# Constants and picked sums in PSUM, a first count split differently between two engines, and GpSimd's second threshold ahead of the spread scales

## The chip, the cores and the metric

The kernel runs on one core of one Trainium2 chip. Its time is the device time of one execution in microseconds (us), and runs of the same kernel are compared by their median. Before the change the median of three runs is 1032.03 us (1031.37 to 1032.18).

A core has five engines that work side by side, each in the order of its own instruction stream: TensorE (PE; the loading of its weights is shown as PEld), VectorE (DVE), ScalarE (ACT), GpSimd (POOL) and SyncE (SP), which here only starts transfers. They wait for each other by counting semaphores. SBUF is the large on-chip memory, PSUM the small one that TensorE writes its products to.

## The reference

Four sequences of 512 tokens with 128 features run through two layers. What matters here is the attention of the second layer: 16 heads, 16 memory keys in front of the 512 tokens, and of the scores of each query only the 64 largest go into the softmax.

```
dots = einsum('bhid,bhjd->bhij', q, k) * scale          # k has 16 memory keys in front
dots = einsum('bhij,hk->bkij', dots, pre_proj)          # heads mixed
dots = where(causal, neg, dots)
top  = lax.top_k(dots, 64)[0]
vk   = top[..., -1:]                                    # the 64th largest score of the row
dots = where(dots < vk, neg, dots)
attn = softmax(dots)
attn = einsum('bhij,hk->bkij', attn, post_proj)
out  = einsum('bhij,bhjd->bhid', attn, v) ... @ Wo + bo
```

Before it come a linear recurrence and a feed-forward part in simulated four-bit numbers, behind it a mixture of eight experts with a shared one. The change does not touch these.

## The kernel before

The work of attention is cut into 64 steps, one for each head of each sequence, numbered g from 0 to 63 (HEADS). In a step the 512 queries are four tiles of 128 rows (t = 0 to 3); because of the causal mask tile t needs only 144, 272, 400 or 528 columns of scores (NT). The mixing of heads is folded into weights ahead of the loop.

What a step does, and on which engine:

- TensorE computes keys (line 415) and scores (lines 438 to 441) of a later head, turns the weights of a head by a product with a scaled diagonal matrix `spread` (`turn_weights`, line 450, 20 matmuls), and multiplies them with the values (`values`, line 464).
- VectorE fetches the scores from PSUM into `Sx` (`fetch`, line 1025), measures their size (lines 1031 and 1036), and counts part of the entries over a first threshold (`tally`, line 1043).
- ScalarE counts the rest of them (`first_tally`, line 728), GpSimd corrects the threshold (`second_threshold`, lines 1313 to 1317), ScalarE counts again for all tiles (`tally`, line 736), and GpSimd corrects once more and shifts the scores by the result (`third_threshold` and `shift`, line 1334). ScalarE counts how many shifted scores are positive (`count`, line 744). The 64th largest score now lies within a few places of zero.
- VectorE finds out which side of zero it lies on (`flip`: `away`, line 1050, `flips`, line 1052, and the flipped scores, line 1056), takes the 8 nearest scores (`nearest`, line 1062), and picks the right one by a mask that GpSimd has made (`pick_last`, lines 1339 to 1344): product with the mask, line 1124, sum, line 1129, flip back into `yk`, line 1134. One matmul of TensorE (`found`, line 471) counts whether each row has its hit; VectorE reads that (`read_hits`, lines 1069 and 1070), and where a row has none it goes through a branch with the next 8 scores (`redo_missed`). `keep` (line 1111) zeroes the softmax weights under the limit and sums the rest; `rinv` (line 1114) is one over the sums.
- GpSimd multiplies the identity by `rinv` into `spread` (`spread_scale`, line 1353) and scales the weights of the memory keys (`mem_w`, line 1357). `turn_weights` waits for `spread`; ScalarE copies its result out of PSUM (`turned_copy`, line 763), and `values` waits for this copy.

The steps overlap: every engine works at several heads at a time. There is no scheduler. Each engine's order is written out in a loop over g with offsets. For ScalarE one pass is: `key_copy(g + 3)`, `tally(g + 1)`, `turned_copy(g - 1)`, `weigh(g + 1)` (the exponentials, line 755), `value_copy(g)`, `count(g + 1)`, `first_tally(g + 2)`. For TensorE: `turn_weights(g - 1)`, `found(g)`, `projected(g)` (line 422), `values(g - 1)`, `scores(g + 3)`, `keys(g + 4)`. For GpSimd: `second_threshold(g + 1)`, `pick_last(g)`, `stage_memory_keys(g + 3)`, `third_threshold(g + 1)`, `shift(g + 1)`, `first_threshold(g + 2)`, and last `spread_scale(g)` with the memory weights.

Of the kernel before, what the change touches and what calls it, by code (L numbers as in the profile page):

```python
# [5 lines left out]
I32 = mybir.dt.int32  # L6
BF16 = mybir.dt.bfloat16
ALU = mybir.AluOpType
# [3 lines left out]
P = 128  # L12
B, T, D = 4, 512, 128
TT = T // P
# [30 lines left out]
def mix_jobs():  # L45

    for i in range(2):
        for lo in range(0, PAIRS, 512):
            yield i, lo, min(PAIRS, lo + 512)
    yield 2, 0, 2 * D  # L50


ORDER = [(b, u) for pair in ((0, 1), (2, 3)) for us in (range(SH), range(SH, UNITS)) for b in pair for u in us]
# [12 lines left out]
def mixed_layers_kernel(nc, xT, W_in, b_in, log_A, B_vec, Cm, Dv, w_gate, w_up, w_down, WqT, WkT, WvT,  # L66
                        pre, post, memkT, memvT, Wo, bo, w12T, w3T, s1T, s2T, s3T, rwT, ebias, steer, outT):
    ctx = ExitStack()
    with ctx:
# [83 lines left out]

        y = [tiles_of(mixed_flat[:, STOT * i:STOT * i + STOT]) for i in range(2)]
        near = tiles_of(mixed_flat[:, 2 * STOT:3 * STOT])
        steer_s = sb("steer_s", [P, 6, TT])
        size = [sb(f"size{i}", [P, TT]) for i in range(2)]
        cf = [sb(f"cf{i}", [P, 5, TT]) for i in range(2)]
        moved = sb("moved", [P, TT])
# [43 lines left out]
        quad = [bA[:, :], bBC[:, 0:512], bBC[:, 512:1024], bI]  # L203
        scores_in = [bA[:, 0:NT[0]], bA[:, OFF[1]:OFF[1] + NT[1]], bBC[:, 0:NT[2]], bBC[:, 512 - MEM:1024]]
        hits_in = bA[0:1, 512 - 2 * TT * WIN:512].rearrange("p (t k) -> p t k", t=TT)
        ln4_bank = [bBC[:, 0:512], bBC[:, 512:1024], bA[:, :], bF]
        half_bank = [(bBC[:, 0:512], bI), (bA[:, :], bBC[:, 512:1024])]
        ln3_bank = [bH[:, :], bF, bG, bI]
# [55 lines left out]
        def _(pe):  # L264
# [306 lines left out]
            for g in range(-2, HEADS + 1):  # L571
                if g == 1:
                    pe.wait_ge(sem("ln_out"), 3 * B)
                if 0 <= g - 1:
                    turn_weights(g - 1)
                if g == HEADS:
                    wide4(0)
                    wide4(1)
                    pe.wait_ge(sem("hits_read"), HEADS)
                    mean4(2)  # L580
                if 0 <= g < HEADS:
                    found(g)
                    projected(g)
                if 0 <= g - 1:
                    values(g - 1)
                if g and g % H == 0:
                    turn_memory(g // H - 1)
                if 0 <= g + 3 < HEADS:
                    scores(g + 3)
                if g + 4 < HEADS:  # L590
                    keys(g + 4)
# [41 lines left out]
        def _(act):  # L633
# [89 lines left out]
            def first_tally(g):  # L723

                act.wait_ge(sem("fetched"), TT * (g + 1))
                act.wait_ge(sem("thr0_ready"), g + 1)
                for t in range(2, TT):
                    last = nc.scalar.activation(unread[1][:, OFF[t]:OFF[t] + NT[t]], Sx[g % 2][:, t, 0:NT[t]], ACT.Sign, bias=cf[g % 2][:, 0, t:t + 1],  # L728
                                                accum_out=above[:, t:t + 1])
                last.then_inc(sem("tallied0_last"), 1)  # L730
# [123 lines left out]
        def _(dve):  # L854
# [184 lines left out]
            def tally(g):  # L1039

                dve.wait_ge(sem("thr0_ready"), g + 1)
                for t in range(2):
                    last = V.tensor_scalar(unread[1][:, OFF[t]:OFF[t] + NT[t]], Sx[g % 2][:, t, 0:NT[t]], cf[g % 2][:, 0, t:t + 1], 0.0, ALU.is_ge, ALU.add,  # L1043
                                           accum_out=above[:, t:t + 1])
                last.then_inc(sem("tallied0"), 1)

            def flip(g):

                dve.wait_ge(sem("counted"), g + 1)
                V.tensor_tensor(away[:, :], over[g % 2][:, :], steer_s[:, 5, :], ALU.add).then_inc(sem("away_ready"), 1)  # L1050
                dve.wait_ge(sem("away_ready"), g + 1)
                V.tensor_scalar(flips[:, :], away[:, :].bitcast(I32), REST, TWO, ALU.bitwise_or, ALU.bitwise_xor).then_inc(sem("flips_ready"), 1)
                dve.wait_ge(sem("flips_ready"), g + 1)
                for t in (3, 2, 1, 0):
                    dve.wait_ge(sem("y_ready"), TT * g + 4 - t)
                    V.tensor_scalar(near[t].bitcast(I32), y[g % 2][t].bitcast(I32), flips[:, t:t + 1], None, ALU.bitwise_xor).then_inc(sem("flipped"), 1)  # L1056
# [15 lines left out]
            def redo_missed(g):  # L1072
# [3 lines left out]
                with dve.If(dve.value_load(hits[0:1, TT:TT + 1]) < TT * P):  # L1076
# [9 lines left out]
                    dve.drain()  # L1086
                    V.tensor_reduce(vk_far[:, :], further[:, :, :], AX.X, ALU.add)
                    dve.drain()
                    V.tensor_tensor(vk[:, :], vk[:, :], vk_far[:, :], ALU.add)
                    dve.drain()  # L1090
                    V.tensor_tensor(yk[:, :].bitcast(I32), vk[:, :].bitcast(I32), flips[:, :], ALU.bitwise_xor)
# [28 lines left out]

            def pick_tops(g):

                dve.wait_ge(sem("topped"), 2 * g + 2)
                V.tensor_tensor(picked_top[:, :, :], pick[:, :, 0:WIN], top[:, :, :], ALU.mult).then_inc(sem("top_picked"), 1)

            def add_tops(g):

                dve.wait_ge(sem("top_picked"), g + 1)
                V.tensor_reduce(vk[:, :], picked_top[:, :, :], AX.X, ALU.add).then_inc(sem("vk_ready"), 1)

            def last_kept(g):

                dve.wait_ge(sem("vk_ready"), g + 1)
                V.tensor_tensor(yk[:, :].bitcast(I32), vk[:, :].bitcast(I32), flips[:, :], ALU.bitwise_xor).then_inc(sem("yk_ready"), 1)  # L1134

            for g in range(-2, HEADS):
                there, coming = 0 <= g, g + 2 < HEADS
                if there:
                    flip(g)
                    nearest(g, (3, 2))  # L1140
                    nearest(g, (1, 0))
                    if g == 0:
                        for b in range(1, B):
                            normed(2, b, ln3_bank[b])
                    if g > H and g % H == 1:
                        take_sum(g // H - 1)
                    read_hits(g)
                if coming:
                    free_for_fetch(g + 2)
                    fetch(g + 2, (0,))  # L1150
                if there:
                    pick_tops(g)
                if coming:
                    fetch(g + 2, (1,))
                if there:
                    add_tops(g)
                if coming:
                    fetch(g + 2, (2,))
                if there:
                    last_kept(g)  # L1160
                if coming:
                    measure_first(g + 2)
                    fetch(g + 2, (3,))
                if there:
# [99 lines left out]
        def _(pool):  # L1264
# [33 lines left out]
            def first_threshold(g):  # L1298

                ph = g % 2  # L1300
                pool.wait_ge(sem("sized"), g + 1)
                if g >= 2:
                    pool.wait_ge(sem("counted"), g - 1)
                Gp.tensor_tensor(cf[ph][:, :, :], size[ph][:, :].unsqueeze(1).broadcast_to((P, 5, TT)), steer_s[:, 0:5, :],  # L1304
                                 ALU.mult).then_inc(sem("thr0_ready"), 1)
                Gp.tensor_scalar(nmax[ph][:, :], rmax[ph][:, :], -1 / DOWN, None, ALU.mult).then_inc(sem("nmax_ready"), 1)

# [38 lines left out]
            def spread_scale(g):  # L1346
# [4 lines left out]
                if g:  # L1351
                    pool.wait_ge(sem("turned_all"), g)
                Gp.tensor_tensor(spread[:, :, :], ident[:, :].unsqueeze(1).broadcast_to((P, TT, P)),  # L1353
                                 r[:, :].unsqueeze(2).broadcast_to((P, TT, P)), ALU.mult).then_inc(sem("spread_ready"), 1)
                if h == 0 and b:
                    pool.wait_ge(sem("memT_done"), b)
                Gp.tensor_tensor(mem_w[:, :, h, :], Ex[g % 2][:, :, 0:MEM], r[:, :].unsqueeze(2).broadcast_to((P, TT, MEM)), ALU.mult).then_inc(sem("mem_ready"), 1)

            for g in range(-3, HEADS):
                if 0 <= g + 1 < HEADS:  # L1360
                    second_threshold(g + 1)
                if g >= 0:
                    pick_last(g)
                if g + 3 < HEADS:
# [6 lines left out]
                if g == -1:  # L1371
                    pool.wait_ge(sem("ln_root"), 1)
                    for b in range(1, B):
                        Gp.tensor_tensor(diag3[b].rearrange("p (t n) -> p t n", t=TT), ident[:, :].unsqueeze(1).broadcast_to((P, TT, P)),
                                         rstd[:, TT * b:TT * b + TT].unsqueeze(2).broadcast_to((P, TT, P)), ALU.mult).then_inc(sem("ln_diag"), 1)
                if g >= 0:
                    spread_scale(g)
            for b in range(B):
                pool.wait_ge(sem("ln_root"), max(b, 1) + 1)
                Gp.tensor_tensor(diag4[b].rearrange("p (t n) -> p t n", t=TT), ident[:, :].unsqueeze(1).broadcast_to((P, TT, P)),  # L1380
                                 rstd[:, TT * b:TT * b + TT].unsqueeze(2).broadcast_to((P, TT, P)), ALU.mult).then_inc(sem("ln_diag"), 1)


def steering():

# [8 lines left out]
    for t in range(TT):  # L1394
        for p in range(P):
# [12 lines left out]
            slope = n * exp(-z * z / 2) / sqrt(2 * pi)  # L1408
            step = sigma / slope
            half = GAIN * step / 2  # L1410
            if t < 2:
# [45 lines left out]
```

## Time and profile before

| | |
|---|---|
| median of 3 runs | 1032.03 us |
| the profiled execution | 1033.08 us, its span 1031.4 us |
| PE busy | 909.6 us (88%) |
| DVE busy | 848.0 us (82%) |
| ACT busy | 746.8 us (72%) |
| POOL busy | 471.8 us (46%) |
| mean granted TensorE clock | 0.950 of full speed |

The span is the time from the first to the last instruction of that execution; what lies around it is 1.7 us. The shares are means over the whole kernel. The loop over heads lies at about 188 to 853 us and has other shares than its surroundings, so it has to be looked at by itself. An engine that is busy all the time within a stretch sets its pace there; where several are, each of them may. In the rows below, "idle before" is the time for which an engine had nothing to do in front of an instruction, and the name behind an arrow is what ended that time.

### The profile page before, as it was taken

What the parts mean: (1) busy time and instruction counts of PE and PEld (TensorE: products, weight loads), DVE (VectorE), ACT (ScalarE), POOL (GpSimd) and SP (SyncE); (2) the same over time, 40 slices, a digit from 0 to 9 for tenths busy, and PEclk for the clock granted to TensorE, in tenths of its full rate; (3) what the DMA queues carried; (4) which work ended last, traced back from release to release, by engine and by line L of the source; (5) the groups of instructions that cost most, each with busy time, mean ns of one, the idle gap of its engine ahead of it and who ended that gap; (6) DMA issues with size and microseconds to landing.
All of it is one profiled execution on the core that took longest, in us unless ns stands there. A gap on an engine that the chain in (4) does not pass through costs nothing.

```text
span 1031.4 us, 16155 instructions
## 1 busy us (share of the span) xinstructions
PE 909.6 (88%) x4151; PEld 581.7 (56%) x4151; DVE 848.0 (82%) x2863; ACT 746.8 (72%) x1932; POOL 471.8 (46%) x1113
## 2 busy tenths in 40 slices
PE   7856777998999998989999999789998789899998
PEld 4523444666666666666666666567666566433432
DVE  4687994999999999999999999989999983446344
ACT  6423236899999999999999999779998883211211
POOL 2000013677676676676766776556765652000000
PEclk9867988899999999999999999989999989899999
DMA  4855310000000000000000000000000000000000
GB/s 155 157 119 92 77 16 1 1 2 2 2 2 2 2 1 2 2 1 2 2 2 2 2 2 2 1 2 2 2 2 1 1 1 1 0 1 10 11 1 21
DMA packets 15006, 18.13 MB, mean 18 GB/s; under 512 B 2657, under 2 KB 12193, under 8 KB 14241
## 3 DMA queue, kind: packets, MB, share of 16 engines
q1 hardware_dynamic: 14880, 16.84, 7.7%
q14 instruction: 93, 0.75, 0.3%
q8 instruction: 33, 0.54, 0.2%
HBM read 11.07 MB, written 5.77 MB: 16 GB/s over the span
## 4 chain that ended last, share of the span: by engine, by line
DVE 48%; PE 28%; issue 11%; ACT 7%; POOL 2%; DVEq 1%; POOLq 1%; DMA 0%; ACTq 0%
DVE Ex L1111 11%; DVE top L1062 7%; DVE mixed L1056 6%; DVE Sx L1025 4%; DVE unread L1043 3%; PE bH L464 3%; DVE yk L1134 2%; PE bFGI L450 2%; PE bBC L559 2%; PE bA L559 2%; DVE away L1050 2%; PE bFGI L568 2%; PE bFGI L560 2%; PE bBC L560 2%; PE bH L568 2%
## 5 line engine op out<-in xcount | busy, mean ns | idle before, releaser
L1334 POOL TENSOR_TENSOR mixed<-Sx,nthr 128x528 f32<-128x528 f32 (+3 forms) x256 | 185.8, 757 | 11.5 <-issue 11.5
L450 PEld LDWEIGHTS bFGI<-spread,Ex 128*128 128x128 f32 x1280 | 157.4, 202 | 58.9 <-POOL spread L1353 57.5
L464 PE MATMUL bH<-turned 128*128 128x512 f32 (+3 forms) x512 | 152.9, 442 | 36.9 <-ACT turned L763 36.6
L450 PE MATMUL bFGI<-spread,Ex 128*128 128x128 f32 x1280 | 166.8, 289 | 17.4 <-POOL spread L1353 17.4
L736 ACT ACTIVATE unread<-Sx,nthr 128x144 bf16<-128x144 f32 (+3 forms) x256 | 143.9, 563 | 20.2 <-POOL nthr L1315 16.6
L464 PEld LDWEIGHTS bH<-turned 128*128 128x128 f32 x512 | 92.1, 189 | 97.9 <-issue 77.6
L744 ACT ACTIVATE unread<-mixed,least 128x528 bf16<-128x528 f32 (+3 forms) x256 | 143.4, 566 | 0.0
L1111 DVE SCALAR_TENSOR_TENSOR Ex<-mixed,yk,Ex 128x144 f32<-128x144 f32 (+3 forms) x256 | 139.5, 598 | 1.7 <-ACT Ex L755 1.0
L755 ACT ACTIVATE Ex<-Sx,nmax 128x144 f32<-128x144 f32 (+3 forms) x256 | 125.5, 563 | 0.0
L1062 DVE MAX8 top<-mixed 128x8 f32<-128x528 f32 (+3 forms) x256 | 110.8, 493 | 0.0
L1353 POOL TENSOR_TENSOR spread<-ident,rinv 128x512 f32<-128x512 f32 x64 | 66.5, 1039 | 84.1 <-DVE rinv L1114 84.1
L728 ACT ACTIVATE unread<-Sx,cf 128x400 bf16<-128x400 f32 (+1 forms) x128 | 85.7, 673 | 9.1 <-POOL cf L1304 9.1
L1056 DVE TENSOR_SCALAR mixed<-mixed,flips 128x528 int32<-128x528 int32 (+3 forms) x256 | 84.0, 390 | 2.3
L763 ACT ACTIVATE turned<-bFGI 128x1280 f32<-128x1280 f32 x64 | 77.8, 1216 | 11.0 <-PE bFGI L450 11.0
L1025 DVE CUSTOM_DVE_ANT_0 Sx<-bBC,causal 128x400 f32<-128x400 f32 (+1 forms) x128 | 79.7, 623 | 0.6 <-PE bBC L441 0.5
L422 PE MATMUL bE<-per_head,xn 128*128 128x128 f32 x512 | 76.9, 295 | 0.0
L441 PE MATMUL bBC<-Y,xn 128*128 128x512 f32 x128 | 71.7, 642 | 0.0
L422 PEld LDWEIGHTS bE<-per_head,xn 128*128 128x128 f32 x512 | 64.6, 198 | 7.9 <-issue 0.9
L415 PE MATMUL bE<-xn,per_head 128*128 128x512 f32 x128 | 65.5, 593 | 1.6 <-DVE xr L986 1.6
L438 PE MATMUL bA<-Y,xn 128*128 128x144 f32 (+1 forms) x256 | 57.4, 348 | 1.4 <-ACT Y L721 0.8
L1290 POOL COPY um_turned<-per_head 128x256 f32<-128x256 f32 x1 | 0.7, 736 | 126.4 <-DMA per_head<-mixed_store 126.4
L839 ACT ACTIVATE Ex<-bBC 128x512 f32<-128x512 f32 x24 | 14.3, 597 | 57.0 <-PE bFGI L560 57.0
(346 smaller groups left out, 1797.7 us busy)
## 6 DMA issues: line engine op xcount, KB each, us to landing
heads_store<-per_head SPq DMA_DIRECT2D x2, 1152.0 KB, 5.0
mixed<-heads_store SPq DMA_DIRECT2D x16, 144.0 KB, 10.8
mixed_store<-mixed SPq DMA_DIRECT2D x2, 1152.0 KB, 4.2
per_head<-mixed_store SPq DMA_DIRECT2D x16, 144.0 KB, 6.0
xr<-in_xT SPq DMA_DIRECT2D x4, 256.0 KB, 3.5
w_s<-in_w12T SPq DMA_DIRECT2D x1, 1024.0 KB, 13.9
outT<-xc SPq DMA_DIRECT2D x4, 256.0 KB, 2.0
wq_s<-in_WqT SPq DMA_DIRECT2D x1, 512.0 KB, 4.2
```

Of the source, the lines that this page charges most:

```text
L422: done = mm(bE[:, jt * P:jt * P + P], xn[:, b, jt * P:jt * P + P], Bw[:, h, :], start=True, stop=True)
L450: last = mm(bFGI[:, k * P:k * P + P], Ex[g % 2][:, t, a:a + P], spread[:, t, :], start=True, stop=True)
L464: last = mm(bH[:, jt * P:T], u[:, jt, :], PT[:, at:at + n], start=h + jt == 0, stop=False)
L728: last = nc.scalar.activation(unread[1][:, OFF[t]:OFF[t] + NT[t]], Sx[g % 2][:, t, 0:NT[t]], ACT.Sign, bias=cf[g % 2][:, 0, t:t + 1], accu ...
L736: last = nc.scalar.activation(unread[0][:, OFF[t]:OFF[t] + NT[t]], Sx[g % 2][:, t, 0:NT[t]], ACT.Sign, bias=nthr[g % 2][0][:, t:t + 1], ac ...
L744: last = nc.scalar.activation(unread[2][:, OFF[t]:OFF[t] + NT[t]], y[g % 2][t], ACT.Sign, bias=least[:, :], accum_out=over[g % 2][:, t:t + 1])
L755: nc.scalar.activation(Ex[g % 2][:, t, 0:NT[t]], Sx[g % 2][:, t, 0:NT[t]], ACT.Exp, bias=nmax[g % 2][:, t:t + 1], scale=1 / DOWN).then_inc ...
L1025: V.tensor_tensor_reduce(out=Sx[g % 2][:, t, 0:NT[t]], in0=scores_in[t], in1=causal[:, W - NT[t]:W], scale=DOWN, scalar=LOW, op0=ALU.add, ...
L1056: V.tensor_scalar(near[t].bitcast(I32), y[g % 2][t].bitcast(I32), flips[:, t:t + 1], None, ALU.bitwise_xor).then_inc(sem("flipped"), 1)
L1062: last = V.max(top[:, t, :], near[t])
L1111: V.scalar_tensor_tensor(Ex[g % 2][:, t, 0:NT[t]], y[g % 2][t], yk[:, t:t + 1], Ex[g % 2][:, t, 0:NT[t]], ALU.is_ge, ALU.mult, accum_out=r ...
L1334: Gp.tensor_tensor(y[ph][t], Sx[ph][:, t, 0:NT[t]], nthr[ph][1][:, t:t + 1].broadcast_to((P, NT[t])), ALU.add).then_inc(sem("y_ready"), 1)
```

## The change

There are three parts, and one thing that follows from them.

First, two operands of small VectorE operations come to lie in PSUM. `steer_p` holds the constants that `away` adds, copied there once ahead of the first head; `vk_p` holds the sums of the picked scores, which `yk` reads. Both lie in the bank `bA`, between the scores of tile 1 and the hits. Because the matmuls of the scores write the same bank, `flip(g)` now also waits until TensorE has done the first scores of head g + 2. The picking and its sum now stand directly behind `read_hits`, ahead of the fetches of head g + 2, and the flip back stands behind the first of the four fetches. In the branch for rows without a hit, the value is rebuilt from `yk` first.

Second, in odd heads VectorE counts three tiles in the first count (0, 1 and 2) and ScalarE one (tile 3). In even heads it stays at two and two. The constants `steer` are given twice, once for each kind of head.

Third, on GpSimd the `spread_scale` and memory weights of head g move from the end of pass g into pass g + 1, behind `second_threshold(g + 2)`.

```diff
+def first_on_vector(g):
+    return 2 + g % 2
...
+        steer_p = bA[:, OFF[2]:OFF[2] + TT]
+        vk_p = bA[:, OFF[2] + TT:OFF[2] + 2 * TT]
...
                 act.wait_ge(sem("thr0_ready"), g + 1)
-                for t in range(2, TT):
+                for t in range(first_on_vector(g), TT):
...
                 dve.wait_ge(sem("thr0_ready"), g + 1)
-                for t in range(2):
+                for t in range(first_on_vector(g)):
...
             def flip(g):
+                if g + 2 < HEADS:
+                    dve.wait_ge(sem("s_done"), 3 * (g + 2) + 1)
                 dve.wait_ge(sem("counted"), g + 1)
-                V.tensor_tensor(away[:, :], over[g % 2][:, :], steer_s[:, 5, :], ALU.add).then_inc(sem("away_ready"), 1)
+                V.tensor_tensor(away[:, :], over[g % 2][:, :], steer_p, ALU.add).then_inc(sem("away_ready"), 1)
...
             def pick_tops(g):
+                dve.wait_ge(sem("pick_ready"), g + 1)
...
-                V.tensor_reduce(vk[:, :], picked_top[:, :, :], AX.X, ALU.add).then_inc(sem("vk_ready"), 1)
+                V.tensor_reduce(vk_p, picked_top[:, :, :], AX.X, ALU.add).then_inc(sem("vk_ready"), 1)
...
-                V.tensor_tensor(yk[:, :].bitcast(I32), vk[:, :].bitcast(I32), flips[:, :], ALU.bitwise_xor).then_inc(sem("yk_ready"), 1)
+                V.tensor_tensor(yk[:, :].bitcast(I32), vk_p.bitcast(I32), flips[:, :], ALU.bitwise_xor).then_inc(sem("yk_ready"), 1)
...
                     read_hits(g)
+                    pick_tops(g)
+                    add_tops(g)
                 if coming:
                     free_for_fetch(g + 2)
                     fetch(g + 2, (0,))
                 if there:
-                    pick_tops(g)
-                if coming:
-                    fetch(g + 2, (1,))
-                if there:
-                    add_tops(g)
-                if coming:
-                    fetch(g + 2, (2,))
-                if there:
                     last_kept(g)
                 if coming:
+                    fetch(g + 2, (1, 2))
                     measure_first(g + 2)
...
             for g in range(-3, HEADS):
                 if 0 <= g + 1 < HEADS:
                     second_threshold(g + 1)
+                if g >= 1:
+                    spread_scale(g - 1)
+                    weigh_memory(g - 1)
                 if g >= 0:
                     pick_last(g)
...
-                if g >= 0:
-                    spread_scale(g)
+            spread_scale(HEADS - 1)
+            weigh_memory(HEADS - 1)
```

On GpSimd, in the middle of the loop, a pass before reads as follows, from the correction of the first threshold of one head (the `cf` made from `size`) to the mask `pick` of the next. `spread` is the diagonal for `turn_weights`, `mem_w` the memory weights, and the three operations on lines 1313, 1315 and 1317 are `second_threshold`:

```order
L1304 TENSOR_TENSOR cf1<-size1,steer_s 128x20
L1306 TENSOR_SCALAR nmax1<-rmax1 128x4
L1353 TENSOR_TENSOR spread<-ident,rinv1 128x512
L1357 TENSOR_TENSOR mem_w<-Ex1,rinv1 128x4x16
L1313 TENSOR_TENSOR moved<-above,cf1 128x4
L1315 TENSOR_TENSOR nthr1_0<-moved,cf1 128x4
L1317 TENSOR_TENSOR cf1<-nthr1_0,cf1 128x4
L1339 TENSOR_TENSOR away2<-away 128x4
L1341 TENSOR_TENSOR pick<-odd2,away2 128x64
```

The same place in the changed kernel, where the line numbers are its own:

```order
L1313 TENSOR_TENSOR cf1<-size1,steer_s 128x20
L1315 TENSOR_SCALAR nmax1<-rmax1 128x4
L1322 TENSOR_TENSOR moved<-above,cf1 128x4
L1324 TENSOR_TENSOR nthr1_0<-moved,cf1 128x4
L1326 TENSOR_TENSOR cf1<-nthr1_0,cf1 128x4
L1362 TENSOR_TENSOR spread<-ident,rinv1 128x512
L1371 TENSOR_TENSOR mem_w<-Ex1,rinv1 128x4x16
L1348 TENSOR_TENSOR away2<-away 128x4
L1350 TENSOR_TENSOR pick<-odd2,away2 128x64
```

The pair of `spread` and `mem_w` has changed places with the three operations of `second_threshold`, the first of which waits for both parts of the first count.

On VectorE, in the changed kernel, this stands between the end of one head and the flip of the next where the count is that of an odd head (`above` are the counts, `rinv` ends the head before):

```order
L1124 RECIPROCAL rinv1<-rsum 128x4
L1049 TENSOR_SCALAR unread1,above<-Sx1,cf1 128x144
L1049 TENSOR_SCALAR unread1,above<-Sx1,cf1 128x272
L1049 TENSOR_SCALAR unread1,above<-Sx1,cf1 128x400
L1058 TENSOR_TENSOR away<-over0,bA 128x4
```

The count over 400 columns is new here; ScalarE had it before.

## Rows read from the trace of the kernel before

**Rows 1.** Windows: stretch, its us; busy us of PE, PEld, DVE, ACT, POOL; PE clock.

```profile
200.00:650.00 450.00, 415.30 (x2217) 294.00 (x2217) 437.08 (x1666) 437.22 (x1183) 313.76 (x746) 1.00 0.01 2
```

**Rows 2.** Timeline (start us, us, engine line), VectorE: `rinv` of heads 13 apart.

```profile
208.36 0.18 DVE L1114 RECIPROCAL rinv<-rsum 128x4 f32<-128x4 f32 x1
...
341.00 0.18 DVE L1114 RECIPROCAL rinv<-rsum 128x4 f32<-128x4 f32 x1
```

**Rows 3.** Timeline of one pass of ScalarE, 500.68 to 510.93 us.

```profile
500.68 1.21 ACT L763 ACTIVATE turned<-bFGI 128x1280 f32<-128x1280 f32 x1
...
506.37 0.62 ACT L728 ACTIVATE unread<-Sx,cf 128x400 bf16<-128x400 f32 x1
...
506.98 0.73 ACT L728 ACTIVATE unread<-Sx,cf 128x528 bf16<-128x528 f32 x1
...
507.60 0.19 ACT L728 ACTIVATION_READ_ACCUMULATOR unread<-Sx,cf 128x1 f32 x1
...
510.93 1.21 ACT L763 ACTIVATE turned<-bFGI 128x1280 f32<-128x1280 f32 x1
```

**Rows 4.** The same pass, GpSimd.

```profile
506.39 1.04 POOL L1353 TENSOR_TENSOR spread<-ident,rinv 128x512 f32<-128x512 f32 x1 [0.91 <-DVE rinv L1114]
...
507.94 0.36 POOL L1313 TENSOR_TENSOR moved<-above,cf 128x4 f32<-128x4 f32 x1 [0.25 <-ACT unread L728]
...
508.81 0.31 POOL L1317 TENSOR_TENSOR cf<-nthr,cf 128x4 f32<-128x4 f32 x1 [0.16 <-issue]
```

**Rows 5.** The same pass, TensorE and its weight loads.

```profile
506.72 1.02 PE L415 MATMUL bE<-xn,per_head 128*128 128x512 f32 x2
...
507.49 2.31 PEld L450 LDWEIGHTS bFGI<-spread,Ex 128*128 128x128 f32 x20 [0.57 <-POOL spread L1353]
...
507.58 2.40 PE L450 MATMUL bFGI<-spread,Ex 128*128 128x128 f32 x20
...
512.29 2.39 PE L464 MATMUL bH<-turned 128*128 128x512 f32 x8 [0.64 <-ACT turned L763]
```

**Rows 6.** The same pass, VectorE.

```profile
500.37 0.16 DVE L1069 TENSOR_REDUCE hits<-bA 1x1 int32<-1x32 f32 x1
...
506.13 0.18 DVE L1114 RECIPROCAL rinv<-rsum 128x4 f32<-128x4 f32 x1
...
506.90 0.08 DVE L1043 DVE_READ_ACCUMULATOR unread<-Sx,cf 128x1 f32 x1
506.90 0.55 DVE L1050 TENSOR_TENSOR away<-over,steer_s 128x4 f32<-128x4 f32 x1
```

**Rows 7.** One line each (min/median/max ns): `yk`, `away`.

```profile
L1134 DVE TENSOR_TENSOR yk<-vk,flips x64: 151/482/902, 183.8 to 849.9; 128x4 int32<-128x4 int32 x64
...
L1050 DVE TENSOR_TENSOR away<-over,steer_s x64: 155/551/553, 176.5 to 845.8; 128x4 f32<-128x4 f32 x64
```

**Rows 8.** Chain of waits (start us, us), behind a late `turn_weights`.

```profile
520.59 2.23 PE bFGI L450 x20
522.82 0.22 PE bA L471 x2
...
523.06 0.07 DVE hits L1069
```

**Rows 9.** Timeline, where `turn_weights` and its copy came late.

```profile
834.69 4.63 PE L450 MATMUL bFGI<-spread,Ex 128*128 128x128 f32 x20 [3.24 <-POOL spread L1353]
...
839.36 1.24 ACT L763 ACTIVATE turned<-bFGI 128x1280 f32<-128x1280 f32 x1 [1.47 <-PE bFGI L450]
```

**Rows 10.** Busy time and granted clock around the wait at 692 us.

```profile
692.00:693.00 1.00, 0.00 (x0) 0.00 (x0) 1.00 (x5) 1.00 (x3) 0.18 (x1) 1.00 0.00 0
...
695.00:696.00 1.00, 1.00 (x6) 1.00 (x7) 1.00 (x3) 0.42 (x3) 0.70 (x4) 0.50 0.00 0
```

**Rows 11.** TensorE's timeline at that place.

```profile
694.74 1.65 PE L450 MATMUL bFGI<-spread,Ex 128*128 128x128 f32 x6 [2.74 <-POOL spread L1353]
```

**Rows 12.** The branch for rows without a hit, all 64 heads.

```profile
L1078 DVE MATCH_REPLACE8 mixed<-top,mixed x12: 285/486/690, 658.1 to 795.1; 128x144 f32<-128x144 f32 x3, 128x272 f32<-128x272 f32 x3, 128x400 f32<-128x400 f32 x3, 128x528 f32<-128x528 f32 x3
```

More of the change, by code:

```diff
@@ L155, in mixed_layers_kernel @@
         near = tiles_of(mixed_flat[:, 2 * STOT:3 * STOT])
-        steer_s = sb("steer_s", [P, 6, TT])
+        steer_s = sb("steer_s", [P, 12, TT])
         size = [sb(f"size{i}", [P, TT]) for i in range(2)]
@@ L578, in _ @@
                     wide4(1)
-                    pe.wait_ge(sem("hits_read"), HEADS)
+                    pe.wait_ge(sem("yk_ready"), HEADS)
                     mean4(2)
@@ L1088, in redo_missed @@
                     dve.drain()
+                    V.tensor_tensor(vk[:, :].bitcast(I32), yk[:, :].bitcast(I32), flips[:, :], ALU.bitwise_xor)
+                    dve.drain()
                     V.tensor_tensor(vk[:, :], vk[:, :], vk_far[:, :], ALU.add)
@@ L1128, in add_tops @@
                 dve.wait_ge(sem("top_picked"), g + 1)
-                V.tensor_reduce(vk[:, :], picked_top[:, :, :], AX.X, ALU.add).then_inc(sem("vk_ready"), 1)
+                V.tensor_reduce(vk_p, picked_top[:, :, :], AX.X, ALU.add).then_inc(sem("vk_ready"), 1)
             def last_kept(g):
                 dve.wait_ge(sem("vk_ready"), g + 1)
-                V.tensor_tensor(yk[:, :].bitcast(I32), vk[:, :].bitcast(I32), flips[:, :], ALU.bitwise_xor).then_inc(sem("yk_ready"), 1)
+                V.tensor_tensor(yk[:, :].bitcast(I32), vk_p.bitcast(I32), flips[:, :], ALU.bitwise_xor).then_inc(sem("yk_ready"), 1)
             for g in range(-2, HEADS):
                 there, coming = 0 <= g, g + 2 < HEADS
+                if g == 0:
+                    V.tensor_copy(steer_p, steer_s[:, 5, :]).then_inc(sem("steer_moved"), 1)
+                    dve.wait_ge(sem("steer_moved"), 1)
                 if there:
@@ L1303, in first_threshold @@
                     pool.wait_ge(sem("counted"), g - 1)
-                Gp.tensor_tensor(cf[ph][:, :, :], size[ph][:, :].unsqueeze(1).broadcast_to((P, 5, TT)), steer_s[:, 0:5, :],
+                Gp.tensor_tensor(cf[ph][:, :, :], size[ph][:, :].unsqueeze(1).broadcast_to((P, 5, TT)), steer_s[:, 6 * ph:6 * ph + 5, :],
                                  ALU.mult).then_inc(sem("thr0_ready"), 1)
@@ L1354, in spread_scale, with weigh_memory @@
                                  r[:, :].unsqueeze(2).broadcast_to((P, TT, P)), ALU.mult).then_inc(sem("spread_ready"), 1)
+            def weigh_memory(g):
+                b, h = divmod(g, H)
+                r = rinv[g % 2]
                 if h == 0 and b:
@@ L1381, in _, with steering @@
                                  rstd[:, TT * b:TT * b + TT].unsqueeze(2).broadcast_to((P, TT, P)), ALU.mult).then_inc(sem("ln_diag"), 1)
-def steering():
+def steering(ph):
     from math import erfc, exp, pi, sqrt
@@ L1410, in steering @@
             half = GAIN * step / 2
-            if t < 2:
+            if t < first_on_vector(ph):
                 out[p, 0:3, t] = z * sigma, AIM * step - z * sigma, -step
@@ L1444 @@
         "rwT": a["L1_ffn_router_w"].T, "ebias": a["L1_ffn_expert_bias"].reshape(1, NE),
-        "steer": steering(),
+        "steer": np.concatenate([steering(0), steering(1)], 1),
     }
```

## The prediction

> **What bounds the kernel now.** I read the page first (spans, shares, the slices, the chain of waits), then the busy time in windows to find a stretch of the loop over heads in which nothing special happens, then the timeline of one pass, one engine at a time. The reader is to see this: between 200 and 650 us VectorE and ScalarE are both busy 97% of the time (437 of 450 us each), TensorE 92%, GpSimd 70%, at the full clock [rows 1]. Thirteen heads take 341.00 - 208.36 = 132.64 us, 10.20 us each [rows 2]. So two engines are full and a third nearly. A small saving on one of them alone is worth little, and a new wait between them costs nearly its full length. What matters is therefore less the busy time than the ring of waits that leads from one head to the next.
>
> That ring runs through `turn_weights` of TensorE. Call T the moment at which it ends for one head. In the pass of the rows it is 507.58 + 2.40 = 509.98 us [rows 5]. Three consumers follow: ScalarE's `turned_copy`, which starts at 510.93 [rows 3], so it has 0.95 us of slack; TensorE's own `found` and with it VectorE's `read_hits`, with a few tenths of slack; and the values behind the copy. On the other side, `spread` starts 0.26 us after `rinv` (506.13 to 506.39), and the weight loads of `turn_weights` 0.06 us after `spread` has ended (507.43 to 507.49) [rows 4 to 6]. TensorE waited 0.57 us there, so `spread` is on time, but not early.
>
> **The first part: operands in PSUM.** `away` takes 0.55 us at the median and `yk` 0.48, and each 0.15 at the least [rows 7]. Both are tiny, so the difference is waiting inside the instruction: `away` at 506.90 ends when `spread` on GpSimd ends [rows 4, 6]. With an operand in PSUM I expect 0.15 to 0.2 us for both, a saving of 0.4 + 0.33 = 0.73 us of VectorE per head. The reordering of picks and fetches adds no instruction; the one copy of constants ahead of head 0 and one operation in the branch are under 1 us in all. The new wait of `flip` for the scores of g + 2 stalls the flips, the 8 nearest and `read_hits` if it is not met; the scores stand ahead of the keys on TensorE, which start at 506.72, before the flip at 506.90 [rows 5, 6], so it costs nothing.
>
> On the lock the Trainium skill says ("SBUF — State Buffer", "Who interferes with whom") that VectorE and GpSimd share one pair of SBUF ports, and that a `tensor_tensor` with both inputs in SBUF contends for it with reads of GpSimd. The trace agrees (0.55 against 0.155 us). A rule that speaks against the change stands in "VectorE: DVE Perf Modes", "The TRN2 errata": the fixed part is 120 cycles with a PSUM source against 58 with an SBUF source; at the 0.96 GHz given there that takes back an estimated 0.13 us per head for the two operations. By it the saving would be 0.60 instead of 0.73. No row shows these two with a PSUM operand.
>
> **The second part: one more tile on VectorE in odd heads.** ScalarE loses the 400-column count, 506.98 - 506.37 = 0.61 us [rows 3], in every second head. VectorE gains a count of 400 columns. `rinv` and the two counts of 416 columns take 506.98 - 506.13 = 0.85 us together [rows 6]; I take 0.6 for the new one. Net, VectorE wins 0.73 - 0.3 = 0.43 us per head and ScalarE 0.3.
>
> **The third part: spread behind the second threshold.** This decides. `second_threshold` waits for both halves of the first count, and ScalarE ends its half at 507.60 + 0.19 = 507.79; `moved` starts at 507.94 and the last of the three operations ends at 508.81 + 0.31 = 509.12 [rows 3, 4]. Only then may `spread` start: 2.73 us later than today's 506.39. Behind it are queued the memory weights, `pick_last`, the third threshold and the shift; waiting for it are `turn_weights`, and through it the copy, `found` and `read_hits`. Against slacks of 0.95 us and a few tenths this becomes the new ring:
>
> - ScalarE's copy starts 0.04 us behind T (834.69 + 4.63 = 839.32 to 839.36, a place where it waited) [rows 9].
> - From the start of the copy to the end of the first count ScalarE is busy without a gap: 507.79 - 500.68 = 7.11 us in an even head, 7.11 - 0.61 = 6.50 in an odd one [rows 3].
> - 0.15 us to `moved` and 1.18 us for the three operations (507.79 to 507.94 to 509.12), then 1.04 for `spread` [rows 3, 4].
> - 0.06 us to the weight loads, and 509.98 - 507.49 = 2.49 us to the end of `turn_weights` [rows 4, 5].
>
> An even head: 0.04 + 7.11 + 0.15 + 1.18 + 1.04 + 0.06 + 2.49 = 12.07 us. In an odd head VectorE's half is the later one. `read_hits` starts 0.24 us behind T (522.82 to 523.06) [rows 8]; from there to `rinv` it is 506.13 - 500.37 = 5.76 us [rows 6], less some 0.65 for the `yk` that no longer waits (its wait in that very pass; at the median it is 0.33 [rows 7]); then 0.85 + 0.6 for the three counts. That is T + 6.8 against ScalarE's T + 6.54, and the head takes 6.8 + 0.15 + 1.18 + 1.04 + 0.06 + 2.49 = 11.7 us. The mean is 11.9, against 10.2: +1.7 us per head. The swap works on 61 heads (from the last two there is no second threshold in front), so +104 us. Where today a head is held up anyway, part of the new wait lies under it: the branch ran in three heads (12 replacements of four tiles each [rows 12]) and three sequences end within the loop. I take 4 us off: **+100 us**. VectorE's 0.43 and ScalarE's 0.3 us are already in the ring where they lie on it; nothing more comes of them, since both engines now have idle time.
>
> **TensorE's clock.** In the new rhythm the values start 0.04 + (512.29 - 510.93) = 1.40 us behind T [rows 3, 5]. In a pass of 10.25 us the values began at 502.04 and the keys ended at 506.72 + 1.02 = 507.74, 5.7 us later [rows 5], so TensorE is done at T + 7.1. The next weight loads come at T + 9.6 (even) or T + 9.2 (odd). It idles 2.5 or 2.1 us in a row in every head, where now it is well below 1. After a wait of 2.74 us behind `spread` the granted clock was 1.0 in the wait and 0.50 behind it (1.2 instead of 2.4 GHz) [rows 10, 11], and after 3.24 us `turn_weights` took 4.63 us instead of 2.40 [rows 5, 9]. A cold `turn_weights` adds 2.2 us to the ring at its full length. The bounds are none (0 us) and all 61 (+134 us). The even heads' 2.5 lies near the 2.74 that did it, the odd ones' 2.1 further off; I take a bit over a third of the heads, 23 x 2.2 = **+50 us**.
>
> **The sum.** 1033.1 (the profiled execution: span and 1.7 us around it) + 100 + 50 = 1183 us; it lay 1 us above the median of the runs shown, so 1182.
>
> **Rivals.**
> (a) The clock stays up. For it: in 450 us of the loop with short gaps it never fell [rows 1], and 2.1 to 2.5 us have no row. Against: the fall after 2.74. Time: 1132 us.
> (b) Nearly every head's turn is cold. For it: the wait recurs in each head. 1033 + 100 + 110 to 134: about 1255.
> (c) The shift is swallowed in part: ScalarE or VectorE gets ahead of the others and the first count ends earlier against `rinv` than in the row. For it: the relief of both engines. Against: the copy that feeds ScalarE's pass itself hangs on `turn_weights`, so it can't run ahead. With half of the 1.7 us left and no cold turns: 1033 + 52 = 1085.
> (d) The other side, faster. By the skill's rule on the shared port pair the first part alone shortens VectorE, the full engine. As a mechanism of this kernel: `spread` is not held up, because `second_threshold` is done by the time `rinv` is; the loop is then paid by ScalarE, 0.3 us less per head, 61 x 0.3 = 18: 1014 us. It decides from the point at which the last threshold operation ends no later than 0.4 us after `rinv` (0.95 with ScalarE's slack alone); in the trace it is 509.12 - 506.13 = 2.99 us [rows 4, 6], and 0.6 less in odd heads.
>
> **How the numbers follow.** Forecast 64%, (a) 19%, (b) 5%, (c) 8%, (d) 4%. The forecast's own span is from some 12 to 35 cold turns, 1158 to 1209. Down to (a) and a little under it, for an odd head that is shorter than I reckon, the range is 1122 to 1212; (b), (c) and (d) stay out. A difference under 0.2% (2 us) can't be told from none. Faster 4%, same 1%, slower 95%.
>
> **What would show it.** In the changed profile: `rinv` every 11.7 to 12.1 us, alternating, plus 2 in the cold ones; `spread` idle before it by the line of `cf` or of the count instead of `rinv`, starting about 3 us behind `rinv`; large idle times of ScalarE's copy on `turn_weights`, of VectorE's `hits` on `found`, and of the weight loads on `spread` above 2 us in nearly every head; ScalarE and VectorE under 88% busy in the loop; `away` and `yk` below 0.25 us; 0.5 in TensorE's granted clock in many slices. The prediction is wrong if `spread` starts within 1 us of `rinv`, or if the copy still finds its input waiting.

## The result and the profile after

The changed kernel takes 1221.93 us at the median of four runs (1217.35 to 1227.04), against 1031.84 us for the kernel before beside it: a ratio of 1.184 (95% interval 1.182 to 1.186). It is slower by 190 us. I had forecast slower, 1182 us with a range of 1122 to 1212, so the sign was right and the size was not; the range missed by 10 us.

The profiled execution took 1227.04 us, its span is 1225.3 us. First the windows and the lines of the page that answer to [rows 1, 7] and show the new waits (columns as there: busy us of PE, PEld, DVE, ACT, POOL, the granted clock, and two for DMA; in the page's part 5 busy us and mean ns, then the idle time in front and what ended it):

```profile
200.00:850.00 650.00, 529.04 (x2405) 389.08 (x2403) 484.30 (x1880) 465.31 (x1236) 333.17 (x804) 0.88 0.00 1
```

```profile
L456 PE MATMUL bFGI<-spread,Ex 128*128 128x128 f32 x1280 | 249.8, 380 | 161.0 <-POOL spread L1362 161.0
...
L769 ACT ACTIVATE turned<-bFGI 128x1280 f32<-128x1280 f32 x64 | 79.2, 1237 | 193.2 <-PE bFGI L456 193.2
...
L1077 DVE TENSOR_REDUCE hits<-bA 1x1 int32<-1x32 f32 x64 | 11.5, 179 | 194.0 <-PE bA L477 194.0
...
L1362 POOL TENSOR_TENSOR spread<-ident,rinv 128x512 f32<-128x512 f32 x64 | 69.9, 1093 | 9.5 <-DVE rinv L1124 9.3
```

No engine is full any longer: VectorE 75% (484 of 650), ScalarE 72%, TensorE 81%. ScalarE's copy waited 193 us for `turn_weights` in 64 heads, VectorE's `hits` 194 us for the matmul behind it, and `turn_weights` for `spread`. `spread` itself shows almost no wait for `rinv`, which was long there. The matmuls of `turn_weights` take 380 ns in the mean where it was 289, and the granted clock of the stretch is 0.88; it was 1.00 in [rows 1], and 0.98 over 200 to 850 us of the kernel before. Line by line, `yk` and `away` did what was forecast (min/median/max ns):

```profile
L1145 DVE TENSOR_TENSOR yk<-bA,flips x64: 155/156/163, 187.5 to 1047.9; 128x4 int32<-128x4 int32 x64
```

```profile
L1058 DVE TENSOR_TENSOR away<-over,bA x64: 151/153/159, 181.5 to 1043.9; 128x4 f32<-128x4 f32 x64
```

Two passes of the changed kernel, from its timeline, answer to [rows 2 to 6]; first one with the count of an odd head, then one with that of an even head:

```profile
491.01 4.13 PE L456 MATMUL bFGI<-spread,Ex 128*128 128x128 f32 x20 [2.45 <-POOL spread L1362]
...
495.37 0.18 DVE L1077 TENSOR_REDUCE hits<-bA 1x1 int32<-1x32 f32 x1 [4.18 <-PE bA L477]
...
495.61 0.43 DVE L1135 TENSOR_TENSOR picked_top<-pick,top 128x32 f32<-128x32 f32 x1
...
500.79 0.18 DVE L1124 RECIPROCAL rinv<-rsum 128x4 f32<-128x4 f32 x1
...
502.27 0.20 POOL L1322 TENSOR_TENSOR moved<-above,cf 128x4 f32<-128x4 f32 x1 [2.69 <-DVE unread L1049]
...
503.39 1.13 POOL L1362 TENSOR_TENSOR spread<-ident,rinv 128x512 f32<-128x512 f32 x1
```

```profile
504.58 4.13 PE L456 MATMUL bFGI<-spread,Ex 128*128 128x128 f32 x20 [2.31 <-POOL spread L1362]
...
508.74 1.24 ACT L769 ACTIVATE turned<-bFGI 128x1280 f32<-128x1280 f32 x1 [3.28 <-PE bFGI L456]
...
508.95 0.18 DVE L1077 TENSOR_REDUCE hits<-bA 1x1 int32<-1x32 f32 x1 [2.68 <-PE bA L477]
...
514.36 0.18 DVE L1124 RECIPROCAL rinv<-rsum 128x4 f32<-128x4 f32 x1
...
515.68 0.20 ACT L734 ACTIVATION_READ_ACCUMULATOR unread<-Sx,cf 128x1 f32 x1
...
516.03 0.38 POOL L1322 TENSOR_TENSOR moved<-above,cf 128x4 f32<-128x4 f32 x1 [2.87 <-ACT unread L734]
...
517.04 0.20 POOL L1326 TENSOR_TENSOR cf<-nthr,cf 128x4 f32<-128x4 f32 x1 [0.16 <-issue]
...
517.20 1.04 POOL L1362 TENSOR_TENSOR spread<-ident,rinv 128x512 f32<-128x512 f32 x1
...
518.29 4.13 PE L456 MATMUL bFGI<-spread,Ex 128*128 128x128 f32 x20 [2.45 <-POOL spread L1362]
```

Read as the ring of the prediction, the even head first, with T = 504.58 + 4.13 = 508.71: the copy starts 0.03 us later (forecast 0.04); from there to the end of the first count 515.88 - 508.74 = 7.14 (7.11); to `moved` 0.15 (0.15); from there to the start of `spread` 1.17 (1.18); `spread` 1.04, and 0.05 to the turn. Every link up to here is within 0.03 us. Only the last is off: `turn_weights` takes 4.13 us where the sum had 2.49, and the head 13.71 us.

In the odd head T is 491.01 + 4.13 = 495.14, and VectorE's half is the later one, as forecast (`moved` waits for its count). But from `hits` to `rinv` it takes 5.42 us where the sum had 5.11, and the next turn starts at T + 9.44 instead of T + 9.2. Most of that is `picked_top`, with two operands in SBUF: 0.43 us here, 0.17 at the same step in the kernel before. Over all heads its mean went from 210 to 379 ns.

### The profile page after: what moved, and what is told of

Its sections match the earlier page's. It is cut to its first block, busy times and chain, and to the rows that moved or that the text cites. A ratio compares the mean times of both kernels' runs of the same rounds, so it can differ in the third digit from the quotient of the medians.

```text
span 1225.3 us, 16288 instructions
## 1 busy us (share of the span) xinstructions
PE 999.0 (82%) x4151; PEld 662.6 (54%) x4151; DVE 854.5 (70%) x2931; ACT 734.0 (60%) x1868; POOL 466.4 (38%) x1113
## 4 chain that ended last, share of the span: by engine, by line
PE 40%; ACT 28%; issue 11%; DVE 9%; POOLq 9%; POOL 2%; DVEq 1%; ACTq 0%; DMA 0%
PE bFGI L456 20%; ACT unread L750 10%; ACT Ex L761 9%; ACT unread L734 5%; POOLq L1349 5%; ACT turned L776 2%; POOLq L1325 2%; PE bBC L565 2%; PE bA L565 2%; PE bFGI L574 2%; PE bFGI L566 2%; PE bBC L566 2%; POOLq L1323 1%; PE bH L574 1%; POOL cf L1326 1%
## 5 line engine op out<-in xcount | busy, mean ns | idle before, releaser
L456 PE MATMUL bFGI<-spread,Ex 128*128 128x128 f32 x1280 | 249.8, 380 | 161.0 <-POOL spread L1362 161.0
L456 PEld LDWEIGHTS bFGI<-spread,Ex 128*128 128x128 f32 x1280 | 237.3, 288 | 212.5 <-POOL spread L1362 210.9
L1343 POOL TENSOR_TENSOR mixed<-Sx,nthr 128x528 f32<-128x528 f32 (+3 forms) x256 | 182.8, 746 | 11.6 <-issue 11.6
L1077 DVE TENSOR_REDUCE hits<-bA 1x1 int32<-1x32 f32 x64 | 11.5, 179 | 194.0 <-PE bA L477 194.0
L1121 DVE SCALAR_TENSOR_TENSOR Ex<-mixed,yk,Ex 128x144 f32<-128x144 f32 (+3 forms) x256 | 129.8, 562 | 1.7 <-DVE yk L1145 1.0
L1064 DVE TENSOR_SCALAR mixed<-mixed,flips 128x528 int32<-128x528 int32 (+3 forms) x256 | 111.2, 497 | 2.5 <-DVE flips L1060 0.2
L1313 POOL TENSOR_TENSOR cf<-size,steer_s 128x20 f32<-128x20 f32 x64 | 17.5, 273 | 197.2 <-DVE size L1042 197.2
L1322 POOL TENSOR_TENSOR moved<-above,cf 128x4 f32<-128x4 f32 x64 | 16.4, 256 | 180.5 <-DVE unread L1049 91.8
L1362 POOL TENSOR_TENSOR spread<-ident,rinv 128x512 f32<-128x512 f32 x64 | 69.9, 1093 | 9.5 <-DVE rinv L1124 9.3
L734 ACT ACTIVATE unread<-Sx,cf 128x528 bf16<-128x528 f32 (+1 forms) x96 | 66.1, 691 | 10.2 <-POOL cf L1313 10.2
```

The source lines that it names most:

```text
L456: last = mm(bFGI[:, k * P:k * P + P], Ex[g % 2][:, t, a:a + P], spread[:, t, :], start=True, stop=True)
L1121: V.scalar_tensor_tensor(Ex[g % 2][:, t, 0:NT[t]], y[g % 2][t], yk[:, t:t + 1], Ex[g % 2][:, t, 0:NT[t]], ALU.is_ge, ALU.mult, accum_out=r ...
L1343: Gp.tensor_tensor(y[ph][t], Sx[ph][:, t, 0:NT[t]], nthr[ph][1][:, t:t + 1].broadcast_to((P, NT[t])), ALU.add).then_inc(sem("y_ready"), 1)
```

## The experiments

Ratios are against the kernel before, run beside each on the same chip.

**e1: the swap alone**, on the kernel before. The diff is that of the third part of the change.

> The kernel before with the third part of the change alone: spread scales and memory weights behind the second threshold. Theory R (the new ring): the swap makes the whole loss. Without the tile that VectorE took over, every head has the longer ScalarE part, 12.1 us warm, and nearly every turn_weights runs cold as in the changed kernel, 1.7 us more. Rinv every 13.6 to 13.8 us, time 1215 to 1240 us. Rival P (the operands in PSUM and their new wait on the scores, or the third count on VectorE, carry a part of the loss): clearly under 1200 us here.

Measured: 1207.6 us, ratio 1.171 (1.168 to 1.173). The swap makes the loss, but the time is some 7 us under the expectation, and 14 us under the changed kernel. `rinv` comes every 13.46 us at most places, with shorter heads between, not every 13.6 to 13.8.

**e2: the change without the swap.**

```diff
-                if g >= 1:
-                    spread_scale(g - 1)
-                    weigh_memory(g - 1)
...
+                if g >= 0:
+                    spread_scale(g)
+                    weigh_memory(g)
```

> The changed kernel with spread scales and memory weights back at the end of GpSimd's pass. Theory R: the loss is gone and the first two parts pay what was reckoned, ScalarE's 0.3 us a head: 1010 to 1025 us, rinv every 9.9 us. Rival P: the new wait of flip on the scores, or PSUM operands, cost something by themselves: at or above 1032 us.

Measured: 1025.6 us, ratio 0.9939 (0.9922 to 0.9955). No cost hides in the first two parts, but the gain is 6 us over 64 heads, about 0.1 us each, not the 0.3 that I had reckoned; `rinv` comes after 10.01 and 10.25 us in turn, not every 9.9. Two things are seen where the rest should be. On ScalarE the 0.61 us of the count that it lost come back as a wait in the same heads: in 22 of the 44 passes between 200 and 650 us its next copy `Y` waits 0.6 us for TensorE's keys, and in no pass of the kernel before. In that stretch of e2:

```profile
ACT Y L727 <- PE bE L421: 13.2, 22, 0.6
```

(us in total, times, longest us.) So TensorE, 92% busy, is the third engine of this loop. On VectorE part of the saving goes into other operations; these are its groups over all heads, `keep` before and in this kernel:

```profile
L1111 DVE SCALAR_TENSOR_TENSOR Ex<-mixed,yk,Ex 128x144 f32<-128x144 f32 (+3 forms) x256 | 139.5, 598 | 1.7 <-ACT Ex L755 1.0
```

```profile
L1121 DVE SCALAR_TENSOR_TENSOR Ex<-mixed,yk,Ex 128x144 f32<-128x144 f32 (+3 forms) x256 | 151.5, 644 | 1.7 <-DVE yk L1145 1.0 <-ACT Ex L761 0.7
```

`yk` and `away` give back 27.6 and 23.9 us in 64 heads (from means of 588 and 526 ns to 157 and 154), but `keep`, with two operands in SBUF like the old `yk`, takes 12.0 us more, and the new count 32 x 0.62 = 20 us. About 20 us of VectorE's time are left, and the time moved by 6.

**e3: TensorE's idle time filled**, in the changed kernel with the swap:

```diff
+                if 3 <= g < HEADS:
+                    for _ in range(5):
+                        mm(bFGI[:, 1280:1536], xn[:, 3, 0:P], xn[:, 3, 0:2 * P], start=True, stop=True)
                 if 0 <= g - 1:
                     turn_weights(g - 1)
```

> The changed kernel with five matmuls of 256 columns in TensorE's idle time ahead of turn_weights, into an unused part of PSUM (their result is not read): about 2.1 us of work in a gap of 2.1 to 2.5 us. Theory C (cold clock in every head makes 1.7 us of the 3.5 us that a head got longer): the clock stays at full, turn_weights takes 2.4 us again, rinv every 11.8 to 12.1 us, time 1115 to 1135 us. Rival W (the excess over my sum is waiting elsewhere, not the clock): the time stays within 1% of the changed kernel's 1222 us or gets longer by the added matmuls.

Measured: 1140.9 us, ratio 1.105 (1.102 to 1.108). TensorE got more to do and the kernel became 81 us faster; it is still 6 us over the 1135 that I had expected at the most. Windows, TensorE's timeline and `rinv` of this kernel:

```profile
200.00:730.00 530.00, 517.58 (x2658) 379.18 (x2659) 439.40 (x1720) 431.77 (x1147) 307.91 (x749) 1.00 0.01 2
```

```profile
307.82 2.32 PE L582 MATMUL bFGI<-xn 128*128 128x256 f32 x10
310.28 2.50 PE L456 MATMUL bFGI<-spread,Ex 128*128 128x128 f32 x20
```

```profile
306.35 0.18 DVE L1127 RECIPROCAL rinv<-rsum 128x4 f32<-128x4 f32 x1
...
318.27 0.18 DVE L1127 RECIPROCAL rinv<-rsum 128x4 f32<-128x4 f32 x1
...
330.07 0.18 DVE L1127 RECIPROCAL rinv<-rsum 128x4 f32<-128x4 f32 x1
```

The clock is 1.00 for 530 us, `turn_weights` is back at 2.50 us, and the heads take 11.92 and 11.80 us in turn, 11.86 in the mean. The prediction's ring at the full clock had 12.07 and 11.7, 11.9 in the mean. The heads of 11.92 are those with ScalarE's longer part (even), those of 11.80 the odd ones, so one was reckoned 0.15 us too long and the other 0.1 too short. Theory C holds, rival W falls.

**e4: only the memory weights behind the second threshold**, `spread` in its old place.

> As the kernel without the swap, but the memory weights alone stand behind the second threshold, since nothing urgent waits for them. If the second threshold waits for GpSimd in odd heads (its half of ScalarE's count ends 0.6 us earlier there), up to 0.25 us of ScalarE's wait in every second head goes: 1000 to 1020 us, at best 8 us under the kernel without the swap. If VectorE paces that kernel, the same time within 3 us.

Measured: 1026.4 us, ratio 0.994 (0.992 to 0.996), no difference from e2. The threshold was not what e2 waited for.

**e5: the swap alone, filled**, as e3 on e1.

> The kernel before with the swap alone and the five filling matmuls ahead of turn_weights (their result is not read). Theory C (the ring of waits is about 11.9 us a head, the rest of the loss is the cold clock): a full clock, turn_weights 2.4 to 2.5 us, rinv every 11.7 to 12.1 us, 1130 to 1145 us, within 10 us of the changed kernel with the same filling (1141 us); the longer ScalarE part in odd heads and the shorter VectorE part about cancel. Rival: the first two parts of the change lengthen the warm ring too, since the changed kernel (1222) is slower than the swap alone (1208): then clearly under 1130 us here.

Measured: 1152.9 us, ratio 1.119 (1.115 to 1.122), 12 us over e3; I had allowed 10, and 1145 us at the most. So at the full clock the first two parts shorten the swapped ring by some 0.2 us per head. At the falling clock they do not: 1222 against 1208.

**e6 and e7: one and three filling matmuls** instead of five.

> The changed kernel with one filling matmul of 256 columns (0.43 us) in front of turn_weights, which leaves TensorE idle for about 1.9 to 2.0 us there. Theory C: if this is still long enough, most turns stay cold and the time stays at 1200 to 1225 us; if the limit lies above it, the clock stays at full and the time falls to 1140 us. I expect in between, 1140 to 1190 us, with fewer cold turns. Rival W (no link between gap and clock): 1222 us within 1%.

> The changed kernel with three filling matmuls (1.3 us in sum), which leaves an idle gap of about 1.1 us. Theory C: at the full clock in every ordinary head, 1135 to 1145 us as with five, since the ring does not run through the filling. Rival F (what counts is how much work is added, not the gap): between one and five matmuls in time, some 1165 us.

Measured: with three 1136.8 us, ratio 1.102 (1.097 to 1.108), the same as with five: rival F falls, since more filling than three matmuls brings nothing. With one, four runs between 1143.4 and 1174.0 us; the spread is itself the finding. In the profile of the run of 1152.5 us the first heads run in one rhythm and later ones in another, with gaps of the same lengths:

```profile
241.94 4.13 PE L456 MATMUL bFGI<-spread,Ex 128*128 128x128 f32 x20 [2.04 <-POOL spread L1365]
...
255.51 4.08 PE L456 MATMUL bFGI<-spread,Ex 128*128 128x128 f32 x20 [1.88 <-POOL spread L1365]
```

```profile
294.44 2.50 PE L456 MATMUL bFGI<-spread,Ex 128*128 128x128 f32 x20 [2.08 <-POOL spread L1365]
...
341.89 2.50 PE L456 MATMUL bFGI<-spread,Ex 128*128 128x128 f32 x20 [1.87 <-POOL spread L1365]
```

Around the first `rinv` is 13.71 us apart (238.01 to 251.72), around the last 11.94 (337.95 to 349.89). Gaps of 1.88 and 2.04 us stood before a late turn, gaps of 1.87 and 2.08 before one at the full clock. So near this length the gap alone does not decide. I sorted the 384 `turn_weights` of the six swapped kernels by TensorE's idle time right in front of them, and counted those over 2.7 us:

| idle in front, us | turns | of them late (over 2.7 us) |
|---|---|---|
| under 0.5 | 119 | 0 |
| 0.5 to 1.8 | 94 | 0 |
| 1.8 to 2.2 | 45 | 19 |
| 2.2 to 2.6 | 98 | 90 |
| over 2.6 | 28 | 27 |

A filling also adds work ahead of the gap that it shortens; no run tells the two apart.

Something else goes with it, and e1 shows what. Three of its turns, then the granted clock inside the second and the third (the clock is the sixth figure behind the comma, leaving out the counts in brackets):

```profile
455.43 4.13 PE L450 MATMUL bFGI<-spread,Ex 128*128 128x128 f32 x20 [2.21 <-POOL spread L1353]
...
509.20 3.67 PE L450 MATMUL bFGI<-spread,Ex 128*128 128x128 f32 x20 [2.33 <-POOL spread L1353]
...
522.26 2.50 PE L450 MATMUL bFGI<-spread,Ex 128*128 128x128 f32 x20 [2.26 <-POOL spread L1353]
```

```profile
509.20:510.20 1.00, 1.00 (x9) 1.00 (x10) 0.12 (x1) 0.97 (x4) 0.70 (x4) 1.00 0.00 0
510.30:512.80 2.50, 2.50 (x13) 2.27 (x12) 0.00 (x0) 0.00 (x0) 2.18 (x6) 0.50 0.00 0
522.30:524.80 2.50, 2.50 (x22) 2.36 (x22) 0.02 (x1) 0.94 (x5) 1.88 (x8) 1.00 0.00 0
```

In e1 the stretches at half clock start at 442.0, 455.7, 469.3, 483.0, 496.6 and 510.3 us, 13.65 us apart. The turns start at 441.97, 455.43, 468.90, 482.36, 495.81 and 509.20 us, 13.45 apart. So each turn lies a little further ahead of the clock's fall, by 0.0 us at first and 1.1 us at the sixth, and has less of the half clock in it: 4.13 us, later 3.92 and 3.67. The seventh escapes it whole, with the same gap of 2.26 us in front, and then it begins anew. In the changed kernel the half-clock stretches are 13.65 us apart too (491.0, 504.7, 518.3, 532.0), but its late heads take 13.57 and 13.71 us in turn, 13.64 in the mean. So the turns (491.01, 504.58, 518.29, 531.86) stay with them.

**e8: the operands in PSUM alone.**

```diff
 def first_on_vector(g):
-    return 2 + g % 2
+    return 2
```

> Only the operands in PSUM with the reordered picks; two tiles each on VectorE and ScalarE in every head, spread scales in their old place. ScalarE keeps its full 10 us of work in every head. Theory S (before and in this kernel ScalarE sets the pace, VectorE's saving only turns into waiting): within 0.4% of before, 1028 to 1033 us. Theory V (VectorE sets the pace): 0.4 us per head net of what comes back as longer keep operations, 1005 to 1020 us, faster than with the third tile on VectorE (1025.6).

Measured: 1031.1 us, ratio 1.001 (0.999 to 1.003), `rinv` every 10.26 us. ScalarE is 97% busy (135.40 of 140 us) and VectorE 95%, with `keep` at 675 ns in the mean: theory S for this kernel. (The figures are from 205 to 345 us.)

```profile
L1121 DVE SCALAR_TENSOR_TENSOR Ex<-mixed,yk,Ex 128x144 f32<-128x144 f32 (+3 forms) x256 | 159.1, 675 | 1.6 <-ACT Ex L761 1.0 <-DVE yk L1145 0.7
```

**e9: the third count on VectorE alone**, without PSUM operands and swap, and **e10: e2 again**, beside it.

> The kernel before with the second part alone: in odd heads the third tile of the first count on VectorE. Theory B (VectorE and ScalarE are both full, so only relief of both helps): VectorE gets 0.3 us a head more and nothing back, ScalarE's 0.3 us turn into waiting, rinv every 10.3 to 10.5 us, 1036 to 1050 us. Theory S (ScalarE alone paces): 1020 to 1027 us, as the kernel without the swap (1025.6).

> The same kernel as e2, the changed one without the swap, beside the one with the third count alone: the ratio to before is 0.994 again, within 0.002, if the gain of 6 us is real.

Measured: e9 1044.0 us, ratio 1.012 (1.010 to 1.015), as theory B has it. Its heads are of two kinds, about 9.9 to 10.4 us and about 11.1 us, and in the long ones the product with the mask meets the start of GpSimd's shift:

```profile
269.88 2.86 POOL L1338 TENSOR_TENSOR mixed<-Sx,nthr 128x528 f32<-128x528 f32 x4 [0.18 <-issue]
269.92 1.07 DVE L1128 TENSOR_TENSOR picked_top<-pick,top 128x32 f32<-128x32 f32 x1
```

An operation on 32 columns takes 1.07 us. The mean over 64 heads is 447 ns; before, at the same place in the order, it was 210, and in e2, where the pick stands directly behind `read_hits`, it is 191. But `yk` and `away` wait less in e9 (442 and 383 ns), and the three together take 81.4 us against 84.7 before. What VectorE has more is the count, 20 us, and that is enough for the 12 us. Theory S alone does not survive this: relieved of the same count, ScalarE waits here for TensorE's keys as in e2 (22 times 0.6 us between 200 and 650 us). Whether it is the PSUM operands or the reordering of the picks, to which I had given no worth, that lets VectorE take the third count in e2 was not tried apart. With the swap the reordering does not keep the pick from waiting (379 ns in the changed kernel).

The repeated e2 gave 1029.3 us, ratio 0.9977 (0.9959 to 0.9994), outside the 0.002 that I had allowed. Both say faster than before, by 0.1% to 0.8% taken together, but the two intervals do not meet, so how much within that stays open. Even so e2 and e4 are the fastest forms here. Of what was tried, the first two parts are worth having only as a pair and without the third.

## Why the prediction was wrong in size

- **The step "spread behind the second threshold" was right.** The links of the even head agree within 0.03 us, the ring at the full clock is 11.86 us against 11.9, and with the clock kept up (e3) the loss over before is 1140.9 - 1032.7 = 108 us against my 100. That the mean fits so well is partly luck: the even head is 0.15 us shorter there than I had it, the odd one 0.1 longer. The 4 us that I took off for heads held up anyway were not saved: by `rinv`, the heads just behind the start of the second and the third sequence grew by 2.8 and 2.3 us in e3 (12.20 to 15.00 and 12.38 to 14.71). The rest I did not split.
- **The step that failed is the number of cold turns in "TensorE's clock".** I took 23 of 61 at 2.2 us, 50 us. Of the changed kernel's 64 turns 55 were late, most at 4.13 us, 1.63 more than 2.50. The mean turn is 3.90 us against 2.62 in e3; 64 x 1.28 = 82 us, and the two kernels stand 1221.9 - 1140.9 = 81 us apart. So far more turns were cold, each for less than the 2.2 us I had. I had placed the odd heads' gap of 2.1 us halfway to safe. It was 2.31 us, because `picked_top` made the odd head's part up to the turn longer (9.44 us against 9.2). And above 2.2 us the turn was late in nine of ten.
- Why so many: I treated the heads as separate draws. They are not. In the changed kernel `rinv` came at 13.57 and 13.71 us in turn for some 25 heads, and of the turns among them one alone, behind a gap of 1.68 us, ran at the full clock. With one filling matmul (e6) that rhythm and the 11.9 us one both stand in one execution, at the same gaps. The rows of e1 show what keeps the rhythm: the stretches at half clock follow one another at 13.65 us, and the heads of the changed kernel, 13.64 us in the mean, keep step with them, while those of e1 slip out. That the two lengths agree is chance as far as the links show, since 13.57 and 13.71 are their sums. What times the fall of the clock itself was not tried. The Trainium skill ("TensorE: Matmul & The Clock Gate", "Part 1: The HAM clock gate") says that the throttled clock is the default and activity releases it; e3 agrees: with more work the clock is 1.00 over 530 us.
- Rival (b), nearly every turn cold, was the right picture, with 5%. Its price of up to 134 us was too high, since the recurring cold turn takes 4.13 us and not the 4.63 of [rows 9]: part of it ran at the full clock.
- **The first part** was right to 0.01 us for the two operations: by the medians they save 0.72 us per head, so the lower 0.60 did not come, and with an operand in PSUM they take 157 and 154 ns in the mean, about what the fastest of before took (151 and 155). Nothing of it reached the time alone (e8): ScalarE was as full, and `keep` took part of it over. **The second part** costs 12 us alone (e9). My rival (d) priced the pair without the swap at 1014 us; it is 1026 to 1029.
- The new wait of `flip` on the scores cost nothing that a row shows.
- Why the changed kernel is slower than e1 although its ring is shorter at the full clock: in e1 49 of 64 turns are late with a mean turn of 3.67 us, fewer and shorter than the 55 and 3.90, because its heads slip against the stretches at half clock. The difference in the means, 64 x 0.23 = 15 us, is as large as the 14 us between the two kernels. No run shifted the length of the head on purpose to test this.

## What to carry to other kernels

Where two or three engines are full, look for the ring of waits and add up its links; a swap of two instructions on an engine that is 46% busy added 1.7 us to every head here, and the mean could be reckoned to 0.04 us, the single head to 0.15. Then ask what the longest idle stretch of TensorE becomes in each pass: in these kernels, with more than about 2.2 us idle in front of the matmuls that everything waits for, they ran late nearly every time, and that cost almost as much as the wait itself. Repeated gaps of one length are not independent: compare the length of the pass with the spacing of the half-clock stretches. Between "never" and "always" the middle is a poor guess; idle time that can't be avoided may be filled with matmuls that nobody reads.

## What the runs showed of the hardware

- A small VectorE operation with both inputs in SBUF ended with the GpSimd operation that ran beside it (1.07 us for 32 columns beside a shift of 528 columns in e9); with one input in PSUM `away` and `yk` took 0.15 to 0.16 us each time. Freed time partly comes back as waiting in the next operation with two SBUF inputs (`keep` 598 ns in the mean before, 644 in e2 and 675 in e8; `picked_top` 210 before, 379 in the changed kernel).
- With 1.8 to 2.2 us of idle time in front 19 of 45 turns ran partly at half clock, above 2.2 us 117 of 126, and below 1.8 us none of 213.
- The stretches at half clock came 13.65 us apart in e1 and in the changed kernel, in e1 against heads of 13.45 us; so they did not follow the gap by a fixed delay.
- Three filling matmuls (1.5 us, leaving a gap of 0.9) were as good as five (2.3 us).
